# Mixture-of-experts tail of an attention kernel: answers scattered to the output by expert instead of gathered by token in a stage of its own

## The reference, cut to what matters

```python
# t: [2, 4096, 256], the residual stream;  h = layernorm(t), as [8192, 256]
idx = argmax(softmax(h @ gate_w + gate_b));  prb = that probability
pos = number of earlier tokens with the same expert;  kept = pos < 1280
buf = zeros(8, 1280, 256);  buf[idx, pos] = h          # dropped where pos >= 1280
y = relu(buf @ w1 + b1) @ w2 + b2                      # per expert, inner size F = 1024
y_tok = y[idx, min(pos, 1279)] * prb * kept
out = t + nan_to_num(y_tok, nan=0, posinf=1e4, neginf=-1e4)
```

## Time and profile before

| | us |
|---|---|
| median of 3 runs (lowest, highest) | 10331.16 (10326.96, 10343.2) |
| the profiled execution, its own time | 10341.0 |
| its span, first to last instruction | 10339.2 |
| PE busy | 7631.7 (74%) |
| DVE busy | 5293.7 (51%) |
| POOL busy | 5133.8 (50%) |
| ACT busy | 3754.9 (36%) |
| TensorE's granted clock, mean | 0.858 |

### The profile page before, as it was taken

How to read it: one execution, slowest core, us unless ns; L and a number is a source line. 1 busy time by engine, 2 the same in 40 slices (tenths; PEclk the granted TensorE clock), 3 DMA queues, 4 the chain that set the end, 5 groups by cost and what they waited for, 6 DMA issues and landing times. The chain is left out here.

```text
span 10339.2 us, 94511 instructions
## 1 busy us (share of the span) xinstructions
PE 7631.7 (74%) x30870; PEld 3966.5 (38%) x30870; DVE 5293.7 (51%) x9576; ACT 3754.9 (36%) x5426; POOL 5133.8 (50%) x4768
## 2 busy tenths in 40 slices
PE   7623326654893799879999687978996999855894
PEld 3612213442442344334444233433442444333563
DVE  7555544564664566556666455656632666421003
ACT  2100002310561366526666244635663455400221
POOL 1078875676776677767777576767500000002003
PEclk9866667877896799979999888988998999966997
DMA  3854335675543555455454445545412111142223
GB/s 128 310 140 107 108 106 162 205 257 178 154 132 117 157 145 140 130 150 147 131 145 134 152 143 159 142 136 154 129 37 77 53 47 46 33 117 93 69 75 108
DMA packets 680981, 1331.69 MB, mean 129 GB/s; under 512 B 173223, under 2 KB 417980, under 8 KB 665376
## 3 DMA queue, kind: packets, MB, share of 16 engines
q0 software_dynamic: 229632, 631.22, 22.0%
q1 hardware_dynamic: 432480, 619.58, 19.5%
q10 hardware_dynamic: 18432, 75.51, 1.8%
HBM read 1018.55 MB, written 307.68 MB: 128 GB/s over the span
## 5 line engine op out<-in xcount | busy, mean ns | idle before, releaser
L660 POOL DMA_INDIRECT sa_slot<-s_table,sa_rec x4608 | 4942.4, 1073 | 2462.7 <-issue 1413.8
L1572 PE MATMUL a_ctx<-a_p,a_v 128*64 128x512 f32 x6400 | 1740.3, 622 | 177.6 <-issue 177.6
L1659 DVE CUSTOM_DVE_ANT_0 a_above<-a_late,a_above 128x512 f32<-128x512 f32 x1600 | 1105.6, 691 | 1449.9 <-PE a_late L1517 1381.0
L1591 ACT ACTIVATE a_p<-a_s 128x1024 f32<-128x1024 f32 x1600 | 1629.9, 1019 | 154.6 <-PE a_s L1555 154.0
L1600 ACT ACTIVATE a_above<-a_diff 128x512 f32<-128x512 f32 x1600 | 956.2, 598 | 1855.9 <-PE a_diff L1505 1820.1
L815 PE MATMUL sa_sums<-keep_ident,sa_vals 128*128 128x128 f32 x4608 | 711.5, 305 | 759.4 <-DVE sa_vals L758 759.4
L1505 PE MATMUL a_diff<-a_kd,a_q 96*128 96x512 f32 x1600 | 840.4, 525 | 277.7 <-DMA a_q<-s_q 256.0
L1555 PE MATMUL a_s<-a_q,a_k 98*128 98x512 f32 x3200 | 1042.6, 407 | 0.0
L815 PEld LDWEIGHTS sa_sums<-keep_ident,sa_vals 128*128 128x128 f32 x4608 | 581.5, 157 | 1171.7 <-DVE sa_vals L758 774.5
L706 DVE TENSOR_TENSOR sa_slot<-sa_slot,sa_q 128x1152 f32<-128x1152 f32 x512 | 693.5, 1354 | 613.7 <-DMA sa_slot<-s_table,sa_rec 613.7
L2155 POOL MEMSET x_ctx<- 128x2 f32 x2 | 0.2, 101 | 1802.2 <-POOLq L74 1802.2
(11 more groups left out here) (272 smaller groups left out, 7922.5 us busy)
## 6 DMA issues: line engine op xcount, KB each, us to landing
sa_slot<-s_table,sa_rec POOLq DMA_INDIRECT x4608
s_table<-t_rows ACTq DMA_DIRECT2D x64, 1024.0 KB, 7.5
a_q<-s_q SPq DMA_DIRECT2D x160, 384.0 KB, 4.4
s_part<-a_o SPq DMA_DIRECT2D x160, 256.0 KB, 2.5
t_qwin<-s_dwq SPq DMA_DIRECT2D x64, 512.0 KB, 6.0
t_kvwin<-s_dwkv SPq DMA_DIRECT2D x64, 386.0 KB, 12.1
a_kd<-s_kd SPq DMA_DIRECT2D x128, 192.0 KB, 4.1
a_o<-s_part SPq DMA_DIRECT2D x96, 256.0 KB, 2.7
```

What stands on the lines that cost most here:

```text
L660: pool.indirect_dma_start(out=self.slot[g][:, k, :, :, :].rearrange("p c a n -> p (c a n)"), out_offset=None, in_=self.s["table"][n // TIL ...
L1572: mm = pe.matmul(self.ps_ctx[i * 2 * HD:(i + 1) * 2 * HD, :], self.v_and_ones(run.head, kb), self.p[slot % P_SLOTS][:, i * CHUNK:(i + 1) * ...
L1591: act.activation(self.p[slot % P_SLOTS][:, :], self.ps_s[slot % 2], ACT.Exp, scale=float(HD) ** -0.5).then_inc(self.exped, 1)
L1659: dve.tensor_tensor_reduce(above, self.ps_late, above, 1.0, LOWEST, ALU.add, ALU.max, self.pair_max[:, t, j:j + 1]).then_inc(self.late_got, 1)
```

## The change

Rows of `buf` grow from 256 to ROW = 264 numbers: the token's 256, its probability, its number plus one, and six zeros. The zero fill at the start and the tiles that hold rows grow with them. The mixing stage stores x twice, to `t2` and to the output, one behind the other on SP. The experts' stage now works out from the number in each row where that row's answer belongs. A row that holds no token gets a number beyond the end, one of its own. POOL gathers the residual rows of an expert from `t2`, ten indirect transfers, while the expert before it is computed. ACT scales each tile of y by the probability column. DVE replaces what is not finite and adds the residual row, tile by tile and two tiles behind the tile that PE has just made. POOL scatters each tile to the output, ten more indirect transfers for each expert. The scratch tensor `y`, its stores and the combining stage are gone. A dropped token keeps the residual row that the mixing stage wrote to the output. The loop over the experts is written out.

```diff
+ROW = C + 8
 # prepare_weights
-    zeros = r.sb("zeros", [P, E * CAP // P * C // FILLS])
+    zeros = r.sb("zeros", [P, E * CAP // P * ROW // FILLS])
 # stage_mix, SP
             sp.dma_start(s["t2"][b].rearrange("t p n -> p t n"), x[:, :, :]).then_inc(t_out, 16)
+            sp.dma_start(out[b].rearrange("(t p) n -> p t n", p=P), x[:, :, :]).then_inc(t_out, 16)
...
-            sp.wait_ge(t_out, 16)
+            sp.wait_ge(t_out, 32)
 # stage_route
-        h = r.sb("h", [P, ALL, C])
+        h = r.sb("h", [P, ALL, ROW])
...
-            for tile, name in ((upper, "upper"), (ones, "ones"), (prio, "prio"), (first, "first")):
+            for tile, name in ((upper, "upper"), (ones, "ones"), (prio, "prio"), (first, "first"), (number, "number")):
...
-            sp.dma_start(h[:, :, :], s["h2"].rearrange("b t p n -> p (b t) n")).then_inc(h_in, 16)
+            sp.dma_start(h[:, :, 0:C], s["h2"].rearrange("b t p n -> p (b t) n")).then_inc(h_in, 16)
...
+            t.link(dve.memset(h[:, :, C:], 0.0))
...
-            tt(keep.answer_w[:, :], prob[:, :], kept[:, :], ALU.mult)
+            t.link(dve.tensor_copy(h[:, :, C], prob[:, :]))
+            t.link(dve.tensor_copy(h[:, :, C + 1], number[:, :]))
...
-            t.link(dve.tensor_copy(keep.answer_row[:, :], row[:, :]))
 # stage_experts, SP
+            sp.dma_start(spare[:, :], d["spare"]).then_inc(spare_in, 16)
+            load(0)
+            load(1)
+            for e in range(E - 2):
                 sp.wait_ge(y_made, RT * e + RT)
-                sp.dma_start(s["y"].rearrange("(e t p) n -> e p t n", e=E, p=P)[bass.ds(e, 1)]
-                             .rearrange("a p t n -> p (a t) n"), y[u][:, :, :]).then_inc(y_out[u], 16)
+                sp.wait_ge(scaled, RT * e + RT)
+                load(e + 2)
 # stage_experts, POOL
+            def fetch(e):
+                u = e % 2
+                pool.wait_ge(tokens_made, e + 1)
+                if e >= 2:
+                    pool.wait_ge(res_out[u], 16 * RT * (e // 2))
+                for k in range(RT):
+                    pool.indirect_dma_start(out=res[u][:, k, :], out_offset=None, in_=old,
+                                            in_offset=bass.IndirectOffsetOnAxis(ap=to_token[u][:, k:k + 1], axis=0),
+                                            bounds_check=B * N - 1, oob_is_err=False).then_inc(res_in[u], 16)
+            fetch(0)
+            for e in range(E):
+                u = e % 2
+                if e + 1 < E:
+                    fetch(e + 1)
+                for k in range(RT):
+                    pool.wait_ge(answered, RT * e + k + 1)
+                    pool.indirect_dma_start(out=flat_out, out_offset=bass.IndirectOffsetOnAxis(ap=to_token[u][:, k:k + 1], axis=0),
+                                            in_=res[u][:, k, :], in_offset=None, bounds_check=B * N - 1, oob_is_err=False)\
+                        .then_inc(res_out[u], 16)
 # stage_experts, ACT, behind each expert's relu pieces
+                for k in range(RT):
+                    act.wait_ge(y_made, RT * e + k + 1)
+                    v = y[(RT * e + k) % 4][:, :]
+                    act.activation(v, v, ACT.Copy, scale=x[u][:, k, C:C + 1]).then_inc(scaled, 1)
 # stage_experts, DVE; tokens(e) waits for the rows of expert e and makes to_token in five operations of 128 x 10
+            def answer(e, k):
+                u, v = e % 2, y[(RT * e + k) % 4][:, :]
+                good, big, neg = goods[k % 2], bigs[k % 2], negs[k % 2]
+                if RT * e + k >= 2:
+                    dve.wait_ge(answered, RT * e + k - 1)
+                dve.wait_ge(scaled, RT * e + k + 1)
+                t.inc(dve.tensor_scalar(good[:, :], v, 0.0, 0.0, ALU.mult, ALU.is_equal))
+                t.inc(dve.tensor_scalar(big[:, :], v, 0.0, 1e4, ALU.is_gt, ALU.mult))
+                t.link(dve.tensor_scalar(neg[:, :], v, 0.0, -1e4, ALU.is_lt, ALU.mult))
+                t.link(dve.tensor_tensor(big[:, :], big[:, :], neg[:, :], ALU.add))
+                t.link(dve.copy_predicated(big[:, :], good[:, :], v))
+                dve.wait_ge(res_in[u], 16 * RT * (e // 2 + 1))
+                dve.tensor_tensor(res[u][:, k, :], res[u][:, k, :], big[:, :], ALU.add).then_inc(answered, 1)
+            dve.wait_ge(spare_in, 16)
+            tokens(0)
+            for e in range(E):
+                if e + 1 < E:
+                    tokens(e + 1)
+                for k in range(RT + 2):
+                    if k < RT:
+                        n = RT * e + k
+                        if n >= 4:
+                            dve.wait_ge(answered, n - 3)
+                        dve.wait_ge(y_mm, n + 1)
+                        dve.tensor_tensor(y[n % 4][:, :], ps_y[k % 2][:, 0:C], b2[e % 2][:, :], ALU.add).then_inc(y_made, 1)
+                    if k >= 2:
+                        answer(e, k - 2)
-def stage_combine(nc, d, s, keep, out):
...
```

More of the change, by code:

```diff
@@ L2360, in stage_experts @@
         PIECES = [(a, min(a + CHUNK, CAP)) for a in range(0, CAP, CHUNK)]
-        x = [r.sb(f"x{i}", [P, RT, C]) for i in range(2)]
+        x = [r.sb(f"x{i}", [P, RT, ROW]) for i in range(2)]
         w1 = [r.sb(f"w1{i}", [P, CH, F]) for i in range(2)]
@@ L2367, in stage_experts @@
         mid = r.sb("mid", [P, FT, CAP])
-        y = [r.sb(f"y{i}", [P, RT, C]) for i in range(2)]
+        y = [r.sb(f"y{i}", [P, C]) for i in range(4)]
+        res = [r.sb(f"res{i}", [P, RT, C]) for i in range(2)]
+        goods = [r.sb(f"good{i}", [P, C], U32) for i in range(2)]
+        bigs, negs = ([r.sb(f"{n}{i}", [P, C]) for i in range(2)] for n in ("big", "neg"))
+        spare, empty, token = r.sb("spare", [P, RT]), r.sb("empty", [P, RT]), r.sb("token", [P, RT])
+        to_token = [r.sb(f"to_token{i}", [P, RT], U32) for i in range(2)]
         ps_x = [r.ps(f"ps_x{i}", [P, 512]) for i in range(2)]
@@ L2377, in stage_experts @@
         XS, MS = RT, FT * len(PIECES)
[L2378 removed]
+        flat_out = out.rearrange("b n c -> (b n) c")
+        old = s["t2"].rearrange("b t p n -> (b t p) n")
         @block.sync
         def _(sp):
[L2382 to L2386, removed]
[L2387 to L2405 removed]
@@ new lines, in _ @@
+                for k in range(XS):
+                    act.wait_ge(xT_mm, XS * e + k + 1)
+                    act.activation(xT[:, :, k * P:(k + 1) * P], ps_x[k % 2][:, 0:C].rearrange("p (h n) -> p h n", h=CH),
+                                   ACT.Copy).then_inc(xT_made, 1)
+                if e:
+                    act.wait_ge(y_mm, RT * e)
+                for k in range(MS):
+                    m, (a, z) = k // len(PIECES), PIECES[k % len(PIECES)]
+                    act.wait_ge(m_mm, MS * e + k + 1)
+                    act.activation(mid[:, m, a:z], ps_m[k % 4][:, 0:z - a], ACT.Relu, bias=b1[u][:, m:m + 1]).then_inc(m_made, 1)
@@ L2634, in lay_out @@
         "first": np.tile(CAP * np.arange(E), (P, 1)).astype(f),
+        "number": (np.arange(B * TILES)[None, :] * P + np.arange(P)[:, None] + 1).astype(f),
+        "spare": np.tile(B * N + 1 + np.arange(P)[:, None], (1, CAP // P)).astype(f),
         "ident": np.eye(P, dtype=f),
```

177 lines of the change are left out of this document (63 added, 114 removed).

## The result

The changed kernel takes 10231.16 us in the median of four runs (10209.71 to 10260.98), and the kernel before, on the same chip, 10337.08 (10326.96 to 10343.2). The ratio is 0.9903, with a 95% interval of 0.9879 to 0.9927: 1% faster, 105.9 us. The forecast was 108.6 us less. The profiled execution of the changed kernel has a span of 10231.6 us, 107.6 less than the span before. Most steps came out as worked out. Two that the forecast didn't have, each of some 11 us, happened to cancel in this pair of executions, so the close total is better than the reasoning.

The account below looks back on a forecast made before the run. PE bounds the experts' stage; a serial 144.7 us tail without PE follows. Terms -128.6 + 14.0 + 4.4 + 1.6 = -108.6 us, forecasting 10222.6 us against the median of 10331.2; own range 10212 to 10234, with rivals 10204 to 10248.

Parts of the forecast that it names:

- The tail: Behind PE's last product: 144.7 us of gathers, vector work and store become 16.1, giving back 128.6 us.
- Landing and exit: At the kernel's end: the last scatter's landing with the stage's exit takes 7.8 us, bounds 4 and 10.
- The second store: Mixing stage: second 4.19 MB store of x delays h's stores and DVE, 7.0 us per image, +14.0 for two.
- Rival 1: Mixing stage: the second store is hidden, h's stores slip past or stall is taken up; 10208.6 us, chance 0.10.
- Borders: Between experts: the tenth scaling holds ACT 0.63 us longer before the next expert's rows; seven cost +4.4 us.
- PE at 2.4 GHz: Experts' stage: sign of being right, PE's clock stays full with a period of 75.3 us for an expert.
- Small terms: Routing's DVE work, extra constant and load, larger zero fill, longer first rows and scatters: +1.6 us in all.
- The half microsecond at the first load of rows: First load of rows: unaligned 1056-byte rows would need 36.5 beats against 32, an estimated 0.5 us more.
- Rival 2: Second half of an expert: DVE mildly bounds, held 0.95 us a tile by POOL; +18 us, 10241, chance 0.14.
- Rival 3: Same place, decisive: each us DVE passes 3.45 a tile costs 80 us; up to 10448 us, chance 0.03.
- Rival 4: Routing stage: rows of 1056 bytes make 64 POOL scatters a third dearer, 20 us; 10243 us, chance 0.04.
- The range: Whole kernel: the forecast's own range with its terms' bounds, 10212 to 10234 us; with rivals, 10204 to 10248.

Follow-up runs that it names:

- lag_one: Changed kernel with each tile's answer one product behind instead of two; 10227.05 us, ratio 0.9889 to the kernel before.
- one_store: Changed kernel with x stored once, to the output, and residuals gathered from there; 12851.22 us beside 12984.16 for the kernel before, ratio 0.9903.
- store_pool: Changed kernel with the second store of x issued from GpSimd's queue instead of SP's; 12596.53 us beside 12711.66 for the kernel before, ratio 0.9926.
- before_border: Kernel before plus a wait and one spare scaling on ScalarE at each border between experts; 12985.71 us beside 12984.16, ratio 1.0007.
- act_order: Changed kernel with ScalarE's last scaling behind its copies for the next expert; 12887.67 us beside 12984.16 for the kernel before, ratio 0.9919.
- combined_late: Changed kernel with one_store, act_order, lag_one, short_rows and the first gathers held back; 12596.46 us beside 12711.66 for the kernel before, ratio 0.9917.
- short_rows: Changed kernel with rows of 258 floats (1032 bytes) instead of 264 (1056); 10227.81 us, ratio 0.989 to the kernel before.
- double_answer: Changed kernel with the five operations replacing infinities and NaNs done twice per tile; 12931.69 us beside 12984.16 for the kernel before, ratio 0.996.

## Why the prediction was right, step by step

- **The tail**: forecast 16.1 us counted from the last add's start, measured 16.6 (10215.04 to 10231.6), so 128.1 back of 128.6. The parts are off in both directions. An answer is 2.0 us, not 2.3: the operations overlap by up to 0.1 us, for instance 0.28 us at 10217.58 and the next at 10217.79. The scatter's hand-over of 0.8 us from DVE to POOL had no price. Landing and exit are 8.2, not 7.8. lag_one confirms the count of answers.
- **The second store**: +14.0 forecast, +14.1 measured, and one_store gave 14.7 back. DVE came 8.5 us late, not 8.2, and the rest followed. Rival 1, that it hides, is excluded. store_pool shows that the reason given, bytes at a full transfer rate, is the right one; the shared queue, which the prediction also named, isn't needed for it.
- **Borders**: 0.63 us each, as worked out, but partly by luck. ACT's scaling is 0.51 us and not 0.41, so PE's wait at a border grew by 0.70 us (0.96 instead of 0.26); 0.08 of it came back ahead of the middle layer (0.47 instead of 0.55).
- **The step that failed** is "PE at 2.4 GHz" in an expert. I priced the pause at the border for itself and took the clock as given. At three of seven borders the granted clock fell to 1.2 GHz for 6.8 us, 2.77 us each (78.1 against 75.33), 8.3 in all. before_border shows that the pause does it without the rest of the change, and in act_order, without the pause, no border had a fall. Beside it the first expert took 78.06 us instead of 75.65, +2.4: TensorE stood at 1.2 GHz for its first 10.2 us instead of 3.6. Why is open; combined_late shows the late rise with no gather ahead of it.
- **Small terms**: +1.6 forecast, +1.9 measured (2.2 at the start, -0.3 in routing), but in other places. The fill was priced by its bytes, 0 to 0.9 us, and the first load behind it was issued 2.0 us later; short_rows shows that more than the bytes counts. The half microsecond at the first load of rows, by the Trainium skill's page DMA: Bandwidth & Descriptors (How a descriptor splits into AXI transactions), didn't show: from its issue to the first matmul it took 13.0 us before and 12.5 after. Other loads lie in that stretch, so this bounds the effect and doesn't exclude it.
- **Rival 2, DVE as the mild bound**: I wrote that only POOL pays. DVE pays too. L2512 in the changed kernel, its durations in ns (min/median/max), and L2511 beside it:

```profile
L2512 DVE TENSOR_SCALAR e_big<-e_y x80: 273/405/570, 9655.7 to 10219.8; 128x256 f32<-128x256 f32 x80
...
L2511 DVE TENSOR_SCALAR e_good<-e_y x80: 282/283/517, 9655.5 to 10219.6; 128x256 uint32<-128x256 f32 x80
```

48 of the 80 on L2512 take over 0.3 us. All of them start while a scatter of POOL's runs and end 0.12 us behind it, as at 10215.58, where one took 0.49 beside a scatter from 10214.99 to 10215.96; outside the scatters they take 0.29. Seven more start within a scatter and don't grow. The first tensor_scalar of an answer, L2511, also starts within a scatter 56 times and is held only once. And POOL's scatters take 1.12 us in the 16 cases where the tensor_tensor of L2514 was running when they began (at 10218.46), 0.97 to 1.01 else. The Trainium skill's SBUF — State Buffer (Who interferes with whom) says that a vector instruction in a mode that uses both of its ports and a GpSimd instruction exclude each other, the first to issue holding the shared pair to its end, and that a vector instruction with two SBUF inputs contends with a GpSimd instruction that reads SBUF. L2512 agrees with the first half in 48 of 55 cases and L2514 with the second; why L2511 isn't held stays open. The price is 0.12 us a tile in the median, not 0.95, and it vanishes in the 0.85 us that DVE still waits ahead of each add. double_answer shows what lies beyond that: 0.56 us a tile too much cost 50 us.
- **Rival 3** didn't come, with DVE at about 2.6 us a tile. Its price of 80 us for each us past 3.45 is near what double_answer shows (50 us for 0.56), but not by PE waiting for a PSUM buffer: the lag was paid at the borders, and part of the 50 us is the clock. **Rival 4** is excluded by the scatters of 973 ns.
- The sum of the stages without attention is 96.8 us less. The table's remaining -10.8 us is attention, whose edited part is only the fill. Five profiles of kernels with longer rows on chip A reach the mixing stages between 9001.3 and 9017.7 us, the one of the kernel before at 9017.2. A spread of this size is that of executions; whether some part of it is a gain can't be told from one profile of before. The medians leave it open too: 96.8 us is a ratio of 0.9906, inside both intervals. So the forecast's total of 108.6 against 105.9 and 108.1 measured rests on two errors of opposite sign, of 10.7 us (the clock) and about as much (attention). That it came so close is luck.
- **The range**: the prediction's own, 10212 to 10234, isn't what its bounds add up to. With the bounds of the second store, the borders, the answers and the landing it would be about 10197 to 10238.

## What to carry to other kernels

Work that is taken off a stage of its own and put beside a busy PE cost here what the slowest hand-over at the borders cost, so look at what stands ahead of the engine that the next block needs first: moving one 0.51 us scaling behind the next expert's copies brought each border back to 74.7 us and kept the clock up. A pause of TensorE has two prices, its own length (0.63 us) and the clock behind it (2.8 us at about a third of the borders). A second copy of a large tile was paid in bytes from either of the two queues tried; let the later reader use the copy that has to be written anyway.

## What the runs showed that I had not expected

- A pause longer by 0.7 us at a border (PE idle 0.96 us instead of 0.26) was enough for the granted clock to fall to 1.2 GHz for 6.8 us at 17 of 56 borders; at the 28 without it it never fell.
- The same kernel took 10340, 12712 or 12984 us on the three chips. The attention stages had about 2300 us at 1.2 GHz in the first case and 4800 to 5150 in the others.
- On chips B and C the first expert took 80 to 85.5 us in the four kernels with early gathers, with ACT taking pieces of the middle layer only every 3.6 us for a time (12241.33, 12244.91, 12248.50 in one_store). This rhythm is missing in the two with late gathers (77.2 and 79.5 us) and in before_border (76.2), and on chip A in every kernel. That gathers beside loads delay ACT there fits this; no run tried it alone.
- In the zero fill, packets of 5160 bytes were 7 ns dearer than those of 5120, those of 5280 another 4 ns.
